# A retrieval kernel on one core: two blocks' sums moved from adding transfers to plain transfers and GpSimd additions

## What is computed

```python
mask = (sequence_ids != 0)[..., None]
gathered = item_embeddings[jnp.clip(sequence_ids - 1, 0)]
seq_emb = jnp.where(mask, gathered, 0.0)
denom = jnp.maximum(mask.sum(axis=1), 1).astype(seq_emb.dtype)
pooled = seq_emb.sum(axis=1) / denom
user_rep = pooled @ W_rec.T + b_rec
retrieved = item_embeddings[retrieved_indices].mean(axis=1)
concat = jnp.concatenate([user_rep, retrieved], axis=1)
gate = jax.nn.sigmoid(concat @ gate_W.T + gate_b)
fused = gate * user_rep + (1.0 - gate) * retrieved
logits = fused @ proj_W.T + proj_b
```

## Time and profile before

| | |
|---|---|
| median of 3 runs | 2191.24 us |
| the profiled execution | 2189.62 us, its span 2187.9 us |
| TensorE busy (PE) | 2083.3 us, 95% |
| VectorE busy (DVE) | 1598.9 us, 73% |
| GpSimd busy (POOL) | 1123.3 us, 51% |
| ScalarE busy (ACT) | 816.7 us, 37% |
| end of the wait for pass 1's pooled sums on VectorE | 605.70 us |
| the same for pass 2 | 837.00 us |
| granted TensorE clock over the span | 0.972 of full speed |

### The profile page before, as it was taken

How to read it: one execution, slowest core, us unless ns; L and a number is a source line. 1 busy time by engine, 2 the same in 40 slices (tenths; PEclk the granted TensorE clock), 3 DMA queues, 4 the chain that set the end, 5 groups by cost and what they waited for, 6 DMA issues and landing times.

```text
span 2187.9 us, 32073 instructions
## 1 busy us (share of the span) xinstructions
PE 2083.3 (95%) x12762; PEld 1073.9 (49%) x12762; DVE 1598.9 (73%) x1825; ACT 816.7 (37%) x1009; POOL 1123.3 (51%) x830
## 2 busy tenths in 40 slices
PE   5678999999999989998999999999999999999999
PEld 4554555555555544443444444444444444444444
DVE  8998998888888767443587877787868865555554
ACT  5865776444445545424321211232211123212121
POOL 5674552788658874755575656666666700000000
PEclk9559999999999999999999999999999999999999
DMA  8999997999879997877779989878889975667665
GB/s 306 336 232 264 291 332 250 296 259 254 237 232 248 263 290 253 310 240 269 224 263 335 316 293 322 268 266 268 311 299 335 372 235 172 210 217 234 229 223 176
DMA packets 222002, 586.82 MB, mean 268 GB/s; under 512 B 21792, under 2 KB 120992, under 8 KB 218528
## 3 DMA queue, kind: packets, MB, share of 16 engines
q1 hardware_dynamic: 91424, 264.21, 35.7%
q0 software_dynamic: 77632, 218.16, 35.5%
q10 hardware_dynamic: 52800, 102.41, 12.5%
HBM read 448.21 MB, written 136.48 MB: 267 GB/s over the span
## 4 chain that ended last, share of the span: by engine, by line
PE 77%; DVE 7%; POOL 7%; ACT 3%; issue 2%; DMA 2%; DVEq 1%; ACTq 0%; POOLq 0%; SPq 0%
PE pooled_ps L1307 35%; PE pooled_ps L1200 22%; PE count_ps L1307 9%; PE count_ps L1182 6%; PE count_ps L1212 6%; POOL gathered L575 4%; POOL gathered L553 2%; ACT counts L973 2%; DVE row_hots L674 2%; DVE keys L676 1%; DMA row_hots<-ret_dram 1%; ACT counts L967 1%; DMA counts<-pool_dram 1%; DVE recip L689 0%; DVE gathered L716 0%
## 5 line engine op out<-in xcount | busy, mean ns | idle before, releaser
L1200 PE MATMUL pooled_ps<-mid,ring 128*128 128x512 f16 x3136 | 733.1, 382 | 1.7 <-issue 1.7
L553 POOL DMA_INDIRECT gathered<-emb,ret_rows x460 | 567.9, 1234 | 305.6 <-DVE gathered L716 146.2
L1200 PEld LDWEIGHTS pooled_ps<-mid,ring 128*128 128x128 f16 x3136 | 294.4, 98 | 312.0 <-issue 12.0
L1307 PE MATMUL pooled_ps<-counts,keys 128*128 128x500 f16 x1920 | 416.1, 374 | 4.2 <-DVE keys L749 3.3
L575 POOL DMA_INDIRECT gathered<-emb,ret_rows x184 | 344.2, 1871 | 137.3 <-ACT ring L981 64.3
L1307 PE MATMUL pooled_ps<-counts,mid 128*128 128x500 f16 x1920 | 412.7, 374 | 0.6 <-DVE counts L762 0.6
L938 DVE SCALAR_TENSOR_TENSOR ring<-pooled_ps,out_scale,counts 128x500 f32<-128x500 f32 x320 | 234.5, 736 | 230.9 <-PE pooled_ps L1307 227.4
L674 DVE TENSOR_TENSOR row_hots<-pair_columns,keys 128x2048 f16<-128x2048 f16 x256 | 313.0, 1223 | 78.9 <-PE count_ps L1182 77.7
L1182 PE MATMUL count_ps<-keys,row_hots 128*128 128x98 f16 x4096 | 283.9, 226 | 65.4 <-DVE keys L676 50.8
L1096 ACT ACTIVATE counts<-counts,strip_scale 128x2000 f16<-128x2000 f32 x75 | 147.0, 1960 | 509.5 <-PE pooled_ps L1307 269.8
L1182 PEld LDWEIGHTS count_ps<-keys,row_hots 128*128 128x128 f16 x4096 | 253.7, 108 | 145.5 <-DVE keys L676 66.9
(11 more groups left out here) (134 smaller groups left out, 1124.8 us busy)
## 6 DMA issues: line engine op xcount, KB each, us to landing
logits<-ring ACTq DMA_DIRECT2D x100, 1000.0 KB, 6.9
ring<-emb_parts SPq DMA_DIRECT2D x147, 512.0 KB, 5.9
counts<-proj_t SPq DMA_DIRECT2D x75, 1000.0 KB, 5.9
counts<-emb SPq DMA_DIRECT2D x14, 1792.0 KB, 10.5
emb_parts<-ring SPq DMA_DIRECT2D x49, 512.0 KB, 7.0
mid<-emb SPq DMA_DIRECT2D x46, 512.0 KB, 7.1
counts<-proj_b SPq DMA_DIRECT2D x75, 250.0 KB, 4.7
gathered<-emb,ret_rows POOLq DMA_INDIRECT x660, 6.0
```

The costliest lines, as they stand in the source:

```text
L553: pool.indirect_dma_start(slots[group][:, a], None, source, column(block, r * SLOT + a))\
L1200: last = pe.matmul(pooled_ps[:, m], ring_v[:, p % RING, c, part, m * P:(m + 1) * P], cvt[:, p % CVT, c], start=(i == 0 and c == 0 and part ...
L1307: last = pe.matmul(logit_ps[n % BANKS][:, 0:W], fused[g // 2][:, f, k, at_user:at_user + P], strip_parts[:, t % 2, w, k, :], start=(k == 0 ...
```

## The change

Blocks 2 and 3 no longer use adding transfers. Their 50 rows come by plain transfers in 25 rounds of two. The first round goes into `total` (two rows, `gathered[:, 0:2]`), each later one into `more` (`gathered[:, 2:4]`), and GpSimd itself adds `more` onto `total`. With each batch index one round is issued (`gather_rows`); the addition of a round (`add_rows`) comes one index later, ahead of the next round's transfers, which overwrite `more` and wait for it. A last addition of half the size and the store follow (`finish_rows`, `store_lane`). Block 2 takes the indices 3 to 29, block 3 the indices 31 to 57. VectorE's `finish_lane(2)` and `finish_lane(3)` are gone.

```diff
+        total, more = gathered[:, 0:SLOT], gathered[:, SLOT:2 * SLOT]
...
+            def gather_rows(block, r):
+
+                to, landed = (total, total_in) if r == 0 else (more, more_in)
+                if r > 1:
+                    pool.wait_ge(rows_added, (block - LANES) * (pl.rounds - 1) + r - 1)
+                for a in range(SLOT):
+                    pool.indirect_dma_start(to[:, a], None, source, column(block, r * SLOT + a)).then_inc(landed, 16)
+
+            def add_rows(block, r):
+                if r == 1:
+                    pool.wait_ge(total_in, 16 * SLOT * (block - LANES + 1))
+                pool.wait_ge(more_in, 16 * SLOT * ((block - LANES) * (pl.rounds - 1) + r))
+                pool.tensor_tensor(total, total, more, ALU.add).then_inc(rows_added, 1)
+
+            def finish_rows(block):
+                pool.wait_ge(rows_added, (block - LANES + 1) * (pl.rounds - 1))
+                pool.tensor_tensor(total[:, 0], total[:, 0], total[:, 1], ALU.add).then_inc(lane_made, 1)
...
                 if index == 3:
                     store_lane(0)
                     store_lane(1)
-                for turn in range(turns):
-                    if index == 3 + 2 * turn:
-                        if turn == 0:
-                            wait_ret_stored(pool, 0)
-                        gather_lane(2, turn)
-                    if index == 36 + 3 * turn // 2:
-                        if turn == 0:
-                            wait_ret_stored(pool, 2)
-                        gather_lane(3, turn)
-                if index == 35:
-                    store_lane(2)
-                if index == 63:
-                    store_lane(3)
+                for block2, first, behind in ((2, 3, 0), (3, 31, 2)):
+                    step = index - first
+                    if step == 0:
+                        wait_ret_stored(pool, behind)
+                    if 2 <= step <= pl.rounds:
+                        add_rows(block2, step - 1)
+                    if 0 <= step < pl.rounds:
+                        gather_rows(block2, step)
+                    if step == pl.rounds + 1:
+                        finish_rows(block2)
+                        store_lane(block2)
...
-                    if g >= 2 and i == 1:
-                        finish_lane(g)
```

More of the change, by code:

```diff
@@ L315, in pooling_program @@
         pool_stored = sem("pool_stored")
+        total_in = sem("total_in")
+        more_in = sem("more_in")
+        rows_added = sem("rows_added")
         sum_in = [[sem(f"sum_in{s}_{a}") for a in range(LANE)] for s in range(LANES)]
@@ L389, in lane_landed @@
         def lane_landed(block, a):
-            turns = 1 if block < LANES else block - LANES + 2
-            return 16 * turns * len(range(a, K, LANE))
+            return 16 * len(range(a, K, LANE))
         def adds_by_pass(g, i):
@@ L561, in store_lane @@
                 pool.wait_ge(lane_made, block + 1)
-                pool.dma_start(ret_dram[:, block], gathered[:, block % LANES * LANE if block < LANES else 0])\
+                pool.dma_start(ret_dram[:, block], gathered[:, block * LANE if block < LANES else 0])\
                     .then_inc(lane_stored[block], 16)
             def gather_lane(block, turn):
-                lane = block if block < LANES else 0
+                lane = block
                 for n in range(turn * LANE, min(turn * LANE + LANE, K)):
@@ L701, in finish_lane @@
             def finish_lane(block):
-                at = (block if block < LANES else 0) * LANE
+                at = block * LANE
                 for a in range(LANE):
```

## The result

The changed kernel takes 2259.64 us (median of 4 runs, 2256.31 to 2265.24), the kernel before 2191.81 us beside it: 1.0313 of before, 95% interval 1.0288 to 1.0338. The forecast was 2245 us and the range 2194 to 2315. The profiled execution has a span of 2255.0 us, 67.1 more than before.

The account below looks back on a forecast made before the run. GpSimd, already just too slow in pass 2, was taken as the bound: +57 us from its path and -3 from a load wait give +54 on 2189.6, 2243.6; forecast 2245 us for the median, range 2194 to 2315.

Parts of the forecast that it names:

- A: GpSimd's addition of one round in blocks 2 and 3: taken as 2.6 us, ends 1.2 and 4.0.
- T: GpSimd's period per batch index in blocks 2 and 3: 9.8 us used, ends 7.9 and 11.8, wanted 7.9.
- L: Start of a round's second plain transfer to its landing: taken as 5.3 us, ends 4.7 and 5.8.
- the sum: GpSimd's path added up index by index through blocks 2 and 3: pass 2 ends at 894 us against 837.0.
- +57: Forecast delay of pass 2's end in us, from GpSimd's path: 894 against 837.0.
- the 381.4 of the sum: Time in us when GpSimd finishes indices 3 and 4, block 2 having started at 368.55.
- 225.4: Time in us for 23 indices at 9.8 each, forecast alike for block 2 and block 3.
- -3 us from TensorE's wait for `load_ret(0)`: Load issued at about 895 us, when pass 3 begins, lands before step 5; TensorE's 2.9 us wait goes.
- Rival 1: GpSimd keeps pace in blocks 2 and 3 and the time falls by 12 to 2179 us; chance 0.12.
- Rival 2: GpSimd's additions each first wait for a running VectorE operation of 1.2 us: +112, 2303 us; chance 0.22.
- the prediction's last sentence: Sign to look for: VectorE's L716 and L674 lasting longer than 1.23 us mean the engines hinder each other.

Follow-up runs that it names:

- the copy: Changed kernel with each GpSimd addition replaced by a copy of the same 128x1024 elements, one input read instead of two: 1.0054 of before.

## Why the prediction was right

- *GpSimd is the bound in passes 1 and 2, though it is busy only 51%.* Right for the changed kernel, and shown: fills that read nothing and take as long per index gave the same ends of the passes as the additions, and the addition made twice turned 123 us of GpSimd's path into about as much time.
- *"So GpSimd is already just too slow in pass 2"*, of the kernel before. Not so: with block 3 begun earlier and the same work on GpSimd, the stall was gone. The 17.5 us of waiting ahead of L562, which the prediction named only as a side effect, were its source.
- *A = 2.6 us for the addition.* Measured 2.47 in the mean (118.6 us in 48), 2.38 in the median. The bounds held, but one of the rows that gave them did not scale: 1.88 ns per element from the select of 128 elements makes 2.0 us for a one-input operation of 1024, and the copy takes 1.03 to 1.2. The Trainium skill's 4497 ns for 2048 elements ("GPSIMD Engine Reference", section 3.1), halved to 2.25 us, was nearer to the median than my estimate. The 0.1 us for semaphores in T stands in no row.
- *T = L + A + 2.0 = 9.8 us.* Measured 9.89 and 10.06, but made up otherwise. The step "start of the round's second transfer to landing L, 5.3 us" failed as the loop's limit: only 11 of the additions waited for a landing, 18.4 us in all. What fills the index is the issue: four transfers at 1.56 to 1.59 us and 0.3 us each, 7.5 us, and 2.47 of addition make 9.9. I had 1.3 us for an issue, from the kernel before. That the two errors cancelled within an index, so that T came out near 9.8, is luck. They did not cancel between the blocks: the sum put the end of index 32 at 635.6 us and, with its landing of 5.3 us under a cover of 4.5, left 0.8 us to wait. Measured, the last issue of index 32 ends at 637.86, and the first addition then waits 3.35 us for a landing and starts at 641.21.
- *Pass ends at about 625 and 894 us.* Measured 634.86 and 905.93. Pass 2 is +68.9 where the sum had +57. The missing 12 us stand in GpSimd's own path. The first addition comes 1.1 us after the 381.4 of the sum; the 23 indices of block 2 took 2.0 us more than the sum's 225.4, the way to block 3's first addition 31.26 us instead of 28.8, and the 23 indices of block 3 another 6.0 us more than 225.4. From block 3's last addition to the end of pass 2 the sum was right (33.4 us for 33). Of the 10 us that pass 1 came late against the forecast, 3 stand in that path; for the other 7 the prediction shows no working. VectorE held up, which the forecast did not price, is to be seen in pass 1 (TensorE idle for 16.4 of 200 us in 390:590, where it was idle for 1.95 before), but by the table above it does not move the end of the pass except through GpSimd's index.
- *-3 us from TensorE's wait for `load_ret(0)`.* In pass 3, 2.5 us were given back (68.9 to 66.4), but mostly not by this, so that the size held is luck. The wait of the dense layers' line L1230 (L1247 after) for the load fell from 2.9 to 1.9 us only; that of the line ahead of it, L1212 (L1229 after), for VectorE from 2.4 to 0.7. I had not seen that this load also waits for the end of all counting (`quad_counted`): it starts at 923.25 us, where I had it at about 895.
- *Rival 1, GpSimd keeps pace.* It needed T of 8.4; the run without additions had 7.8 and gave 0.9928, which is -16 us, so the rival's arithmetic (-12 us) was about right and its condition was not met.
- *Rival 2, the engines get in each other's way.* The mechanism is there, turned round. I had GpSimd's addition waiting for a running VectorE operation of 1.2 us; the additions last 2334 ns at least, 2382 in the median and 2978 at most, so they hardly wait. It is VectorE's operation that is drawn out from 1.22 to 3.50 us, as the prediction's last sentence had it for this rival. By the interpolation between the fills it costs, with the slower issues next to it, about 20 us of the 67, against the 58 that the rival had put on top.
- *VectorE waiting some 40 us for landings; additions 2.3 to 3 us; starts 9.5 to 10.5 us apart; a lower clock around the ends of the passes; logits unchanged.* All as named: 48.6 us, 2.33 to 2.98, 9.9 to 10.1, a granted clock of 0.86 in 590:640 and 0.90 in 835:880, no change after 1144.63.

## What to carry to other kernels

An engine with half of its time free in the mean can be the one that sets the pace in a stage: count its path for one turn of the loop, issue times and gaps included, and hold it against the rate that the stage needs. Where two engines are both near that rate, work moved from transfers onto one of them costs about its full length there from the point on where the wanted rate is passed, and it can draw out the other's operations besides. Before replacing a slow operation, look for idle time on the same engine just ahead of it: moving one wait and five indices gained 0.6%, about what additions that cost nothing would have given (0.7%).

## What was not expected of the hardware

- VectorE's operations on two SBUF operands wait for the whole length of a GpSimd operation that reads SBUF (1.22 to 3.50 us beside an addition of 2.36; means of 1441 and 1390 ns against 1221 and 970), and not at all for one that only writes (1221 and 970 beside fills of 1.82 us, the longest L697 1227). The Trainium skill ("SBUF — State Buffer", section "Who interferes with whom") states both: a VectorE instruction with two SBUF inputs contends with a GpSimd instruction that reads SBUF, and not with one that only writes it. The trace agrees in both points. That it was nearly always VectorE that waited was not expected: GpSimd's additions varied from 2334 to 2978 ns only. Where two additions followed each other directly, the second was drawn out too, to 2845 ns in the mean and 3359 at most.
- Issuing a plain indirect transfer of 128 rows took 1.25 to 1.28 us in the mean in pass 1 before and 1.56 to 1.59 us after, with no adding transfers left. What goes with it is VectorE's being busy: 0.95 to 0.97 us where it was idle at the start of the issue, 1.50 (before) and 1.59 us (after) in the mean where it was busy, and 1.49 in the run without additions. The cause stays open.
- With no adding transfers about, the DMA share in 390:590 fell from 0.94 to 0.70. Part of that is the slower pace, 220 GB/s for 258 in this stretch; but the run without additions moved 260 GB/s at a share of 0.80. A batch landed sooner, too. L556 in 490:610 of the changed kernel:

```profile
DMA to landing us min/median/max: 3.5/4.3/5.9
```

The median was 5.4 us in the same stretch before, and 5.8 beside adding transfers in pass 2.
